# A graph layer's row gather: rows that SyncE fetched go to GpSimd's indirect gathers

## What is computed

```
h = maximum(layernorm(x), 0)
msg = relu(h[src] + edge_attr)
agg = segment_sum(msg, dst, num_segments=6250)
h = h + agg
h = relu(h @ W1 + b1)
out = x + h @ W2 + b2
```

## Time and profile before

| what | value |
|---|---|
| timed runs, median of 3 (lowest, highest) | 1424.37 us (1424.08, 1425.36) |
| span of the profiled execution | 1718.4 us |
| mean granted TensorE clock in it | 0.952 |
| TensorE matmul busy | 1484.2 us |
| VectorE busy | 1217.8 us |
| ScalarE busy | 1080.4 us |
| GpSimd busy | 1069.0 us |

### The profile page before, as it was taken

The page is one execution under the profiler, slowest core; times in us unless marked ns, Lnnn a source line. Parts: engine busy times, 40 slices in busy tenths (PEclk is TensorE's granted clock), DMA queues, the critical chain, the costliest instruction groups (busy, mean ns, idle before and its releaser), DMA issues.

```text
span 1718.4 us, 25387 instructions
## 1 busy us (share of the span) xinstructions
PE 1484.2 (86%) x7837; PEld 728.7 (42%) x7837; DVE 1217.8 (71%) x1877; ACT 1080.4 (63%) x1180; POOL 1069.0 (62%) x1128
## 2 busy tenths in 40 slices
PE   4788898898889889888898898889988899888897
PEld 2344444444434444444344444444444444444444
DVE  6578677676767767767677667776767766777676
ACT  5585666475655766657566576655756656566572
POOL 7666666666666566666666656666656665666661
PEclk9899999999999999999998999999999999999999
DMA  6222222232222222222222222222222222222220
GB/s 200 50 48 76 48 78 76 53 78 69 56 71 58 76 49 78 73 57 76 52 75 77 52 70 57 76 71 57 78 68 58 78 51 77 49 77 74 55 71 13
DMA packets 68479, 116.08 MB, mean 68 GB/s; under 512 B 32162, under 2 KB 34492, under 8 KB 68340
## 3 DMA queue, kind: packets, MB, share of 16 engines
q1 hardware_dynamic: 31732, 75.95, 14.0%
q0 software_dynamic: 35600, 36.40, 10.8%
q10 hardware_dynamic: 1008, 2.06, 0.3%
HBM read 110.98 MB, written 3.34 MB: 67 GB/s over the span
## 4 chain that ended last, share of the span: by engine, by line
PE 51%; ACT 15%; another core or an unknown queue 13%; DVE 12%; issue 8%; DVEq 1%; POOL 0%; ACTq 0%
PE ps_cand L1223 50%; ACT keyhot L718 7%; ACT keyhot L725 6%; DVE parts L987 3%; DVE picked L932 2%; DVE gath L939 2%; DVE ends L997 2%; DVE ps_edge L980 1%; PE ps L390 1%; ACT agg L698 1%; ACT ps_edge L706 1%; DVEq L1036 1%; DVE agg L1048 0%; ACT agg L689 0%
## 5 line engine op out<-in xcount | busy, mean ns | idle before, releaser
L361 POOL DMA_INDIRECT gath<-h_table,idx_all x1106 | 1052.2, 951 | 610.2 <-issue 297.6
L1223 PE MATMUL ps_cand<-table_hi,keyhot 128*128 128x448 f16 x3444 | 1252.5, 364 | 114.8 <-issue 76.0
L1223 PE MATMUL ps_cand<-table_lo,keyhot 128*128 128x448 f16 x3444 | 1251.0, 363 | 74.0 <-issue 73.8
L932 DVE TENSOR_TENSOR picked<-ps_cand,cand_mask 128x448 f32<-128x448 f32 x496 | 306.0, 617 | 379.5 <-remote 269.6
L718 ACT ACTIVATE keyhot<-key_pair,key_bias 128x512 f16<-128x512 f16 x861 | 539.3, 707 | 48.6 <-remote 28.1
L1223 PEld LDWEIGHTS ps_cand<-table_hi,keyhot 128*128 128x128 f16 x3444 | 344.5, 100 | 473.1 <-issue 162.0
L1223 PEld LDWEIGHTS ps_cand<-table_lo,keyhot 128*128 128x128 f16 x3444 | 344.9, 100 | 423.9 <-issue 144.8
L725 ACT ACTIVATE keyhot<-keyhot,hot_bias 128x3584 f16<-128x3584 f16 x123 | 403.7, 3282 | 4.0
L939 DVE TENSOR_REDUCE gath<-picked 128x64 f32<-128x448 f32 x496 | 303.4, 612 | 4.4
L706 ACT ACTIVATE ps_edge<-edge_pair 128x832 f32<-128x832 f32 x123 | 106.2, 864 | 260.7 <-DVE parts L987 169.0
L987 DVE SCALAR_TENSOR_TENSOR parts<-ps_edge,side 128x832 f32<-128x832 f32 x242 | 235.3, 1014 | 0.0
(11 more groups left out here) (90 smaller groups left out, 186.0 us busy)
## 6 DMA issues: line engine op xcount, KB each, us to landing
edge_pair<-edges_t SPq DMA_DIRECT2D x62, 832.0 KB
gath<-h_table SPq DMA_DIRECT2D x1280, 0.2 KB
gath<-h_table,idx_all POOLq DMA_INDIRECT x1106
key_pair<-key_table SPq DMA_DIRECT2D x61, 256.0 KB
h_table<-xh SPq DMA_DIRECT2D x7, 224.0 KB
part_x<-x_t SPq DMA_DIRECT2D x29, 48.0 KB
out<-part_out SPq DMA_DIRECT2D x29, 48.0 KB
xh<-x_rows ACTq DMA_DIRECT2D x4, 224.0 KB, 5.1
```

The lines of the kernel that those rows point to most:

```text
L361: nc.gpsimd.indirect_dma_start(out=rows[:, r, :], out_offset=None, in_=h_table, in_offset=bass.IndirectOffsetOnAxis(ap=idx[:, r:r + 1], ax ...
L932: nc.vector.tensor_tensor(picked[i][:, :, :], ps_cand[cand_bank(t, u, i)][:, 0:D * CAND].rearrange("p (d b) -> p d b", b=CAND), mask.to_br ...
L1223: last = nc.tensor.matmul(bank[:, 0:D * CAND], keyhot[u % 2][:, a, i * P:(i + 1) * P], half[:, a, :, :].rearrange("p d b -> p (d b)"), sta ...
```

## The change

SyncE fetches no rows of h any more, and its list of row numbers, the wider buffers, two semaphores and the wait for them go. GpSimd gathers nine tiles and TensorE makes four in every chunk. The diff, cut to its core:

```
-ROW_SLOTS = (3, 1)
-ROWS_AT = (16, 6)
-ROWS_A_LOAD = 16
-ROW_TILES = (TURNS - 1) * PAIRS * sum(ROWS_AT) // P
...
 def pool_tiles(t, u):
-    return TILES_PER_CHUNK - pe_tiles(t, u) - row_tiles(t, u)
+    return TILES_PER_CHUNK - pe_tiles(t, u)
...
-        gath_wide = [sb(f"gath{u}", [P, TILES_PER_CHUNK + (u in ROW_SLOTS), D]) for u in range(SLOTS)]
-        gath = [gath_wide[u][:, 0:TILES_PER_CHUNK, :] for u in range(SLOTS)]
-        row_idx = sb("row_idx", [len(ROW_CHUNKS), P], I32)
+        gath = [sb(f"gath{u}", [P, TILES_PER_CHUNK, D]) for u in range(SLOTS)]
...
                 sp.dma_start(key_pair[h][:, :, :].rearrange("p c e -> p (c e)"),
                              key_table[rows].rearrange("c e -> (c e)").partition_broadcast(P)
                              ).then_inc(key_loaded[h], 16)
-                fetch_rows(row_share(t, h, False))
 
                 sp.wait_ge(summed, t * SLOTS + end)
                 sp.dma_start(edge_pair[h][:, :, :, :], edges_t[:, rows, :, :]).then_inc(edge_loaded[h], 16)
-                if h == 0 or t <= FIRST_PART_TURN:
-                    fetch_rows(row_share(t, h, True))
...
-            sp.dma_start(row_idx[:, :], src_rows).then_inc(row_idx_loaded, 16)
...
-            sp.wait_ge(row_idx_loaded, 16)
-            sp.wait_ge(h_stored, 16 * N_GROUPS)
...
-                fetch_rows(row_share(t, PAIRS - 1, True))
...
-                n, m, k = pool_tiles(t, u), pe_tiles(t, u), row_tiles(t, u)
+                n, m = pool_tiles(t, u), pe_tiles(t, u)
                 released = {i * n // m: pe_before(t, u, i) + 1 for i in range(m)}
                 if not alone(t, u):
-                    gather_rows(slot_rows(t, u)[:, k:, :], idx_all[:, t * SLOTS + u, k:], n, gathered[u], released)
+                    gather_rows(gath[u], idx_all[:, t * SLOTS + u, :], n, gathered[u], released)
...
                 dve.wait_ge(gathered[u], 16 * pool_through(t, u))
-                if row_tiles(t, u):
-                    dve.wait_ge(rows_landed[ROW_SLOTS.index(u)], 16 * rows_through(t, u))
-
-                nc.vector.tensor_tensor(edge_near if near(t, u) else edge_sum, slot_rows(t, u),
+
+                nc.vector.tensor_tensor(edge_near if near(t, u) else edge_sum, gath[u][:, :, :],
                                         edge_near if near(t, u) else edge[u], ALU.add).then_inc(summed, 1)
```

More of the change, by code:

```diff
@@ L79 @@
 CAND = GROUP
-ROW_SLOTS = (3, 1)
-ROWS_AT = (16, 6)
-ROWS_A_LOAD = 16
-ROW_TILES = (TURNS - 1) * PAIRS * sum(ROWS_AT) // P
-ROW_CHUNKS = [((-(-P * (k + 1) // sum(ROWS_AT)) - 1) // PAIRS + 1, ROW_SLOTS[k % 2]) for k in range(ROW_TILES)]
 KEY_BLOCKS = N_GROUPS
@@ L104, in pe_tiles @@
     return PE_FIRST[u] if t == 0 else PE_TILES[u]
-def row_tiles(t, u):
-    return int((t, u) in ROW_CHUNKS)
 def pool_tiles(t, u):
-    return TILES_PER_CHUNK - pe_tiles(t, u) - row_tiles(t, u)
+    return TILES_PER_CHUNK - pe_tiles(t, u)
 def pe_before(t, u, i=0):
@@ L120, in pool_through @@
     return sum(pool_tiles(k, u) for k in range(t + 1))
-def rows_through(t, u):
-    return P * (ROW_CHUNKS.index((t, u)) // 2 + 1)
 def cand_bank(t, u, i):
@@ L133, in bank_uses_before, with build @@
     return before - CAND_BANKS + 1 if before >= CAND_BANKS else None
[L136 to L142, removed]
+def build(nc, x_rows, x_t, src_t, src_keys, src_cands, dst_t, base_t, edges_t, w1, b1, w2, b2, out):
     h_table = nc.dram_tensor("h_table", [NODES_PAD, D], F32, kind="Internal").ap()
@@ L309, in build @@
         late_idx_loaded = sem("late_idx_loaded")
-        row_idx_loaded = sem("row_idx_loaded")
-        rows_landed = [sem(f"rows_landed{s}") for s in ROW_SLOTS]
         edge_loaded = [sem(f"edge_loaded{h}") for h in range(PAIRS)]
@@ L349, in build @@
         again_stored = sem("again_stored")
-        def slot_rows(t, u):
-            shift = int(u in ROW_SLOTS and not row_tiles(t, u))
-            return gath_wide[u][:, shift:shift + TILES_PER_CHUNK, :]
         def gather_rows(rows, idx, tiles, signal, released=None):
@@ L471, in _ @@
                              ).then_inc(key_loaded[h], 16)
[L472 to L483, removed]
             def load_pair(t, h):
@@ L605, in gather_chunk @@
                 pool.wait_ge(summed, t * SLOTS + (u + 1))
-                n, m, k = pool_tiles(t, u), pe_tiles(t, u), row_tiles(t, u)
+                n, m = pool_tiles(t, u), pe_tiles(t, u)
                 released = {i * n // m: pe_before(t, u, i) + 1 for i in range(m)}
                 if not alone(t, u):
-                    gather_rows(slot_rows(t, u)[:, k:, :], idx_all[:, t * SLOTS + u, k:], n, gathered[u], released)
+                    gather_rows(gath[u], idx_all[:, t * SLOTS + u, :], n, gathered[u], released)
                     return
                 early = n - END_LATE
-                gather_rows(slot_rows(t, u)[:, m:, :], idx_all[:, t * SLOTS + u, m:], early, gathered[u],
+                gather_rows(gath[u][:, m:, :], idx_all[:, t * SLOTS + u, m:], early, gathered[u],
                             {r: count for r, count in released.items() if r < early})
-                gather_rows(slot_rows(t, u)[:, END_EARLY:, :], idx_all[:, t * SLOTS + u, END_EARLY:], END_LATE, gathered_late,
+                gather_rows(gath[u][:, END_EARLY:, :], idx_all[:, t * SLOTS + u, END_EARLY:], END_LATE, gathered_late,
                             {r - early: count for r, count in released.items() if r >= early})
@@ L938, in add_candidates @@
                 dve.wait_ge(masked, pe_before(t, u, i) + 1)
-                nc.vector.tensor_reduce(slot_rows(t, u)[:, column, :], picked[i][:, :, :], AX_X, ALU.add).then_inc(selected, 1)
+                nc.vector.tensor_reduce(gath[u][:, column, :], picked[i][:, :, :], AX_X, ALU.add).then_inc(selected, 1)
             def window_onehot(t, u):
@@ L1017, in end_sum @@
                     dve.wait_ge(gathered_late, 16 * END_LATE)
-                nc.vector.tensor_tensor(edge_near[:, cols, :], slot_rows(TURNS - 1, u)[:, cols, :], edge_near[:, cols, :], ALU.add
+                nc.vector.tensor_tensor(edge_near[:, cols, :], gath[u][:, cols, :], edge_near[:, cols, :], ALU.add
                                         ).then_inc(summed, 1)
@@ L1354 @@
     src_keys[:N_CHUNKS] = src_pe.reshape(N_CHUNKS, PE_MAX * P)
-    src_rows = np.stack([src.reshape(N_CHUNKS, P, TILES_PER_CHUNK)[t * SLOTS + u, :, 0] for t, u in ROW_CHUNKS])
     dst = np.concatenate([np.asarray(dst), np.asarray(dst)[N_EDGES - 1:].repeat(extra)])
@@ L1364 @@
         "src_t": src.reshape(N_CHUNKS, P, TILES_PER_CHUNK).transpose(1, 0, 2),
-        "src_rows": src_rows,
         "src_keys": src_keys,
```

## The result

The changed kernel takes 1437.41 us (median of 4 runs, 1436.18 to 1437.49), the kernel before 1424.71 us in the same comparison (4 runs, 1424.08 to 1425.36): ratio 1.0088, 95% interval 1.0075 to 1.0100, or 12.7 us more. The forecast was 12.5 us more.

A forecast was written before the change was run, and what follows sets the result against it. The prediction took POOL's serial gathers to bound the timed run. Ten more gathers at 1.249 us add 12.5 us, everything else counted as nothing: 1424.4 + 12.5 = 1436.9 us, range 1428 to 1441 us.

The forecast's parts named there:

- The bound: Timed run bound by POOL's gathers: nine tiles take 11.24 us, PE's chunk 10.95 us, 0.29 less.
- The price: Ten gathers added on POOL's serial queue, 1.249 us each: 12.5 us more, bounds 9.5 to 15.0 us.
- SyncE's rows cost nothing: SP loses 1280 one-row DMAs, some 376 us of its queue, beside other work: nothing gained.
- the profiled span: Profiled execution of the changed kernel: POOL's waits swallow the ten gathers, span stays near 1718 us.
- the way from a late gather to TensorE: Late gather holds DVE's `sum_edges`; behind it stand the next chunk's masks, which free PE's four candidate banks.
- TensorE's chain: PE's matmuls, scatters, layers, transposes and tail, without gaps: 1402.3 us, 13 to 16 us shorter than POOL's.
- POOL's own chain: 1106 gathers at 1.249 us from 22.91 us, a landing of 0 to 2.9 and the tail: 1415.1 to 1418.0 us.
- The rule that spoke against the sum: Issuing DMAs on several engines saves only usually small sequencer time; by it the change costs nothing: 1424.4 us.
- Hidden: Rival, 12%: POOL has room, PE's chain or DVE and ScalarE coupling sets the end; 1424.4 us, within 0.2%.
- partly hidden: Rival, 9%: gather step near 1.23 us, POOL has the last word in part of the turns; 1428 to 1433 us.
- Faster: Rival, 7%: PE binds and SP's row fetching holds it up; without a 12.89 us stall, 1411.5 us.

The follow-up runs named there:

- e3: The changed kernel with twenty chunks of eight gathered tiles, the tiles left out fetched by nobody (1096 gathers): 1417.46 us, ratio 0.9933 to the kernel before.
- e1: The kernel before, with SyncE's rows fetched into a column never summed and GpSimd gathering nine tiles in every chunk: 1439.6 us, ratio 1.0089.
- e2: The changed kernel with the ten tiles SyncE had fetched now fetched by nobody: 1426.42 us, ratio 0.9996 to the kernel before.
- second profile: The kernel before, unchanged, profiled once more: 1423.96 us with a span of 1421.8 us.
- e4: The changed kernel with eight gathered tiles in every chunk of turns 1 to 29 (116 tiles left out, 1000 gathers): 1417.85 us, ratio 0.9937 to the kernel before.
- e7: The kernel before with SyncE fetching 18 tiles in place of 10, 32 and 8 rows a pair of chunks: 1417.81 us, ratio 0.9954.
- e8: The kernel before with SyncE fetching 16 tiles in place of 10, 28 and 8 rows a pair of chunks: 1417.96 us, ratio 0.9956.
- e6: The kernel before with SyncE fetching 16 tiles in place of 10, 26 and 9 rows a pair of chunks: 1455.19 us, ratio 1.0216.

## Why the prediction was right, and where a step was not

**The bound was read rightly, out of steps and not out of shares.** The forecast rested on POOL's chain being longer than PE's by 0.29 us a nine-tile chunk. The steps measured without disturbance are 11.30 and 10.98 us, some 0.3 apart. VectorE's waits for landed gathers (54 in the kernel before, 75 in the changed one, 2 in e3) show where the bound sits in each.

**The price** of ten gathers, 12.5 us from steps of 1.249 us, is the measured 12.7 us; e1 and e2 show that it goes with the gathers alone. That SyncE's rows cost nothing, for which the prediction named the waits at the edge loads as cover, is shown by the same two runs. Without the rows SyncE's waits there grow. In the second profile of the kernel before:

```profile
SPq L498 <- DVE ps_edge L980: 499.5, 60, 21.5
```

and in the changed kernel:

```profile
SPq L456 <- DVE ps_edge L930: 1120.8, 60, 27.6
```

That is 621 us more waiting at the edge loads, and SyncE's other waits grow by some 146 us. The rows' own instructions, summed over the second profile, take 588 us of SyncE's queue, 0.46 us a row: 383 us for the DMAs, the moves and the register operations, which the prediction put at 376, and 205 us for loading the row numbers, which it left out.

**A step that failed: the profiled span.** The prediction said that the span "should stay near 1718 us", since POOL's waits would swallow the ten gathers. (The ordinary spacing in these waits, 151 x 0.30, is 45 us and not 46, which changes nothing.) It fell to 1435.3 us. The step took the gaps on "issue" for something that the profiler does to this kernel; they were one execution's. The other half of that reading, that the timed runs lack them, held, and saved the sum. The test that would have warned was on the page: a kernel whose span is a fifth above its timed median is not showing its timed self.

**A step that failed: the way from a late gather to TensorE.** The prediction let a late gather hold up VectorE's masks, which free TensorE's four banks. In the changed kernel TensorE waits for the masks once, at 2.7 us, as the kernel before does; what it waits for 23 times is ScalarE's keys:

```profile
PE ps_cand L1173 <- ACT keyhot L677: 14.6, 23, 4.7
...
PE ps_cand L1173 <- DVE picked L884: 2.7, 1, 2.7
```

In the second profile of the kernel before the keys were late 6 times, 6.7 us in all. The chain of the changed kernel behind 1050 us gives the way (its longest pieces):

```profile
1051.28 2.52 DMA gath<-h_table,idx_all
1053.89 1.03 DVE ps_edge L930
1055.97 1.87 DVE parts L937 x2
1058.73 4.33 ACT keyhot L670 x7
1063.08 3.29 ACT keyhot L677
1066.42 10.78 PE ps_cand L1173 x56
```

The late landing delays VectorE's sum and the products behind it. ScalarE's copy of the next edge features (L658, 0.87 us, between the products and the keys) waits for these products, 202.0 us in all, and in ScalarE's queue the keys for TensorE stand behind the copy. The price did not hang on this step; it was taken from POOL's own queue.

**A mis-sized term: TensorE's chain,** 1402.3 us in the prediction. The floor in e4 has a span of 1415.3 us, 13 us more. The steady turns explain 29 x (43.94 - 43.78) = 4.6 us of it: 56 candidates in front of another kind of matmul take 10.70 us, where 56 of the prediction's steps make 10.61. The tail was 2 us shorter than counted. The rest, some 10 us, lies in the first two turns, which the prediction counted as gap-free. There TensorE waits 4.69 us for ScalarE's keys, and behind that wait the candidates run at half their rate, as the PE timeline of e4 shows:

```profile
75.51 0.56 PE L1178 MATMUL ps_cand<-table_hi,keyhot 128*128 128x448 f16 x1 [4.69 <-ACT keyhot L682]
...
80.34 0.58 PE L1178 MATMUL ps_cand<-table_lo,keyhot 128*128 128x448 f16 x1
...
81.49 0.35 PE L1178 MATMUL ps_cand<-table_lo,keyhot 128*128 128x448 f16 x1
```

From 75.51 to 80.71 us the granted clock is 0.50 (the level of 1.2 GHz) and the steps are 0.37 us; from 81.30 us on they are 0.19 us again. At 124.33 us TensorE has waited 2.65 us for VectorE's masks, behind VectorE's set-up work, on which the chain of e4 lies from 83.8 us; some ten candidates at the lower level follow there too. The two waits are 7.3 us, and the slower steps add some 4.4 us; that is a little over the rest, as the first candidates also start 0.8 us earlier than counted. So the margin by which POOL bound the kernel before was 6 to 9 us and not 13 to 16. The forecast did not depend on it, since the change moved away from that side; a forecast of the reverse change would have.

**POOL's own chain** was put at 1415.1 to 1418.0 us; the second profile shows 1421.8. The start (22.8 us) was right and the tail half a microsecond shorter. The landing comes 2.5 us behind the start of a gather, that is 1.5 us behind its end, within the 0 to 2.9 us counted there. The mean step is (1408.81 - 22.77) / 1105 = 1.254 us and not 1.249: the usual step is 1.249, but some twenty gathers take 1.0 to 2.5 us in place of 0.95 and add about 6 us. The 2.0 us that the Trainium skill states for a DMA's fixed cost (DMA: Bandwidth & Descriptors, Anatomy of one DMA — SWDGE (gpsimd) path) is about a fifth under the 2.4 to 2.5 us measured here from issue to landing.

**The rule that spoke against the sum** did not decide here. The Trainium skill (DMA: Bandwidth & Descriptors, Issuing engines are not separate DMA queues) says that issuing from several engines saves only sequencer time, usually small. Ten gathers hold GpSimd's queue for 12.6 us in steps of 1.255 us and cost 12.7 us in the timed runs, since VectorE stood waiting for what this queue fetched; between e3 and e4, where it hardly waits, ninety-six gathers are worth nothing. Rule and trace agree once one asks whether the issuing queue is itself the bound.

**The rivals.** Hidden and partly hidden fall with the timed ratio. Faster falls with e1 and e2: the burst of SyncE's rows beside PE's stall was not its owner, for in e1 the rows are there and the stall is not.

## What to carry to other kernels

Read a bound from the step between an engine's instructions, from whether its queue has holes, and from who waits for it. A queue at 75% busy whose longest idle time is 0.3 us is full, but full is not yet the bound: in e3, e7 and e8 POOL's queue has no hole either, VectorE waits for it only 2, 1 and 10 times, and TensorE sets the time. Where two engines are within 3% of each other, the end of the shorter one is the most that relief can bring: here ten gathers cost 12.7 us when added, but taking away any number brings only 6 to 9. And hold a profile's span against the timed runs before using its waits; when they differ by a fifth, profile again.

## What the runs showed of the hardware that was not expected

Loading 16 numbers from SBUF into SyncE's registers took 1.2 us (up to 1.4) where the load started at a multiple of four 4-byte numbers and 3.5 us at any other start (e6, e8, and the second profile of the kernel before). Sixteen row tiles were a loss of 30 us with such starts (e6) and a gain of 6 us without them (e8).

After waits of 4.69 and 2.65 us in the first two turns of e4, TensorE ran for a few microseconds with the granted clock at 0.50, 0.37 us a candidate in place of 0.19.

One profiled execution of an unchanged kernel was 294 us longer than its timed runs, with stalls on several engines at once; the next profile of the same kernel was within 2.1 us of its own timed run.
